# One loop over image pairs for the patch embedding and the first attention of a two-layer ViT

## The reference, cut to what matters

```python
p = x.reshape(n, C, NP, PS, NP, PS).transpose(0, 2, 4, 1, 3, 5).reshape(n, NP * NP, D_IN)
tokens = jnp.einsum('npd,hd->nph', p, W) + b
tokens = jnp.concatenate([cls, tokens], axis=1) + pos_embed[None]
...
h = _layernorm(tokens)                       # of each token, over its 192 features
q, k = h[:, :64], h[:, 64:]                  # the values are the keys
attn = softmax(einsum('bqc,bkc->bqk', q, k) * 0.25)
out = einsum('bqk,bkc->bqc', attn, k)
out = transpose(out, (0, 2, 1)).reshape(B, -1, 192) @ proj_w.T + proj_b
tokens = tokens + concatenate([out, k], axis=1)
```

## Time and profile before

| what | value |
|---|---|
| median of 3 runs | 2829.3 us (2827.83 to 2830.43) |
| the profiled execution, its own time | 2830.04 us |
| its span, first to last instruction | 2828.2 us |
| busy: PE / DVE / ACT / POOL, share of the span | 92% / 84% / 67% / 40% |
| TensorE clock granted, mean | 0.929 of full speed |

### The profile page before, as it was taken

How to read it: one execution, slowest core, us unless ns; L and a number is a source line. 1 busy time by engine, 2 the same in 40 slices (tenths; PEclk the granted TensorE clock), 3 DMA queues, 4 the chain that set the end, 5 groups by cost and what they waited for, 6 DMA issues and landing times. The chain is left out here.

```text
span 2828.2 us, 82965 instructions
## 1 busy us (share of the span) xinstructions
PE 2588.6 (92%) x27416; PEld 2173.2 (77%) x27416; DVE 2378.9 (84%) x5917; ACT 1904.5 (67%) x5750; POOL 1136.9 (40%) x1288
## 2 busy tenths in 40 slices
PE   5797888699999799999999999999999999997776
PEld 5796555477777588888888888888888888885554
DVE  6955666699999688888888888888888888887998
ACT  3343444333333388888888888888888888886998
POOL 5585333222222034334333433433333344344665
PEclk9897555599999999999999999999999999997999
DMA  9461000000000133333333333333333333330111
GB/s 286 137 187 52 0 0 0 0 1 0 0 0 0 27 79 78 73 68 77 69 72 77 77 71 70 77 68 74 77 77 70 71 75 68 75 78 9 42 40 47
DMA packets 181687, 173.31 MB, mean 61 GB/s; under 512 B 19064, under 2 KB 180290, under 8 KB 181379
## 3 DMA queue, kind: packets, MB, share of 16 engines
q1 hardware_dynamic: 181634, 172.64, 25.1%
HBM read 46.68 MB, written 9.68 MB: 20 GB/s over the span
## 5 line engine op out<-in xcount | busy, mean ns | idle before, releaser
L1183 POOL TENSOR_TENSOR b_pr<-b_pr,b_rinv 128x394 f32<-128x394 f32 (+1 forms) x768 | 625.7, 841 | 1008.4 <-DVE b_rinv L1141 1008.4
L1078 ACT ACTIVATE b_pr<-b_banks,b_nmx 128x197 f32<-128x197 f32 (+1 forms) x1536 | 625.0, 423 | 28.2 <-DVE b_nmx L1135 25.6
L1049 ACT ACTIVATE b_pt<-b_bank_t 128x394 f16<-128x394 f32 (+1 forms) x768 | 337.4, 493 | 203.5 <-PE b_bank_t L1014 203.3
L1135 DVE TENSOR_REDUCE b_nmx<-b_banks 128x2 f32<-128x394 f32 (+1 forms) x768 | 397.3, 558 | 64.7 <-PE b_banks L1004 56.5
L1106 DVE TENSOR_TENSOR b_pt<-b_bank_t,b_pt 128x394 f16<-128x394 f32 (+1 forms) x768 | 395.8, 556 | 18.3 <-ACT b_pt L1049 18.2
L988 PE MATMUL b_banks<-b_xt,wqkv 128*128 128x197 f16 x3840 | 373.6, 249 | 4.5 <-DVE b_xt L1106 2.2
L1014 PE MATMUL b_bank_t<-ident,b_pr 128*128 128x128 f32 (+3 forms) x3072 | 341.8, 253 | 3.1 <-DVE b_pt L1106 3.0
L988 PEld LDWEIGHTS b_banks<-b_xt,wqkv 128*128 128x128 f16 x3840 | 320.5, 98 | 25.7 <-issue 18.8
L1004 PE MATMUL b_banks<-b_kst,b_qst 128*128 128x197 f16 (+1 forms) x3072 | 326.9, 248 | 6.8 <-ACT b_pr L1078 5.4
L1078 ACT ACTIVATION_READ_ACCUMULATOR b_pr<-b_banks,b_nmx 128x1 f32 (+1 forms) x1536 | 315.5, 205 | 0.0
L1014 PEld LDWEIGHTS b_bank_t<-ident,b_pr 128*128 128x128 f32 (+3 forms) x3072 | 282.2, 142 | 43.2 <-issue 35.4
(11 more groups left out here) (175 smaller groups left out, 4657.4 us busy)
## 6 DMA issues: line engine op xcount, KB each, us to landing
b_qst<-b_qk SPq DMA_DIRECT2D x512, 147.8 KB, 2.5
b_kst<-b_qk SPq DMA_DIRECT2D x512, 73.9 KB, 2.3
patches<-in_x SPq DMA_DIRECT2D x64, 588.0 KB, 4.4
out<-z_res SPq DMA_DIRECT2D x32, 192.0 KB
out<-z_res SPq DMA_DIRECT2D x32, 103.5 KB
h<-in_wqkv SPq DMA_DIRECT2D x2, 1152.0 KB, 7.6
h<-in_w SPq DMA_DIRECT2D x2, 576.0 KB, 8.1
h<-in_fc SPq DMA_DIRECT2D x1, 768.0 KB
```

The source lines that it names most:

```text
L1049: return nc.scalar.activation(dst, src, ACT.Copy)
L1078: last = nc.scalar.activation(pr[n % 3][0:ROWS[c], c, e, :], banks[0:ROWS[c], c, e * SEQ:(e + 1) * SEQ], ACT.Exp, bias=nmx[n % 2][0:ROWS[c ...
L1135: v.reduce_max(nmx[n % 2][0:ROWS[c], c, :], banks[0:ROWS[c], c, 0:2 * SEQ].rearrange("p (e t) -> p e t", e=2), AX.X, negate=True).then_inc ...
L1183: last = nc.gpsimd.tensor_tensor(p, p, inv, ALU.mult)
```

## The change

`embed_patches` and `attention_0` become one function, `embed_attend`. Each engine has one list of steps for a round; a `'` behind a step means one pair ahead and each `^` one pair behind. A round makes both images of one pair (steps with 0 and 1: `h` the high parts on ACT, `l` the low parts on POOL, `E` the matmuls, `a` the addition of positions, `b` the statistics) and the attention steps of earlier pairs. Parts and token banks are one per image of a pair instead of four.

`norm_tables` is no longer called for this stage. In its place stand steps `r0` to `r14` on DVE for each pair, on tiles of 128 x 4: four `bn_aggr`, then a guess of the inverse root by integer arithmetic and three Newton steps, and the scale and offset for ACT. POOL no longer adds keys: ACT does it with an activation in place (`u`), `scale` 1 + 1/sigma (`u` for the 133 key rows of each of the two images, four activations). The projection's bias comes from one more matmul. The weight jobs stand after `a1` (or `a0`) of pairs 3, 5, 7, 8 to 10, 10, 12 and 14. More small loads stand ahead of the first image.

```diff
-        embed_patches(nc, A, S, n_img)
-        attention_0(nc, S, n_img)
+        embed_attend(nc, A, S, n_img)
...
+    PE_ORDER = "E0 t^^^^ x^^^ j^^^^^ m^^^^ E1 s^^^".split()
+    ACT_ORDER = ("u^^^ h0' k^^^ g^^^^ x^^ e^^^ h1'").split()
+    DVE_ORDER = ("o^^^^^ r8^^ r9^^ r10^^ t^^^^ r11^^ r12^^ r13^^ i^^^^ b1^ r14^^ n^^ s^^^^^^ r0^ a0 f^^^^^ "
+                 "r1^ r2^ r3^ m^^^ r4^ r5^ x^^ p^^^ b0 a1 r6^ r7^").split()
...
-        patches = [sb(f"patches{b}", [P, PATCH_K, SEQ]) for b in range(BUF)]
-        parts = [sb(f"parts{b}", [P, 2, PATCH_K, SEQ + 1], F16) for b in range(BUF)]
-        tokens = [ps(f"tokens{b}", [P, 512]) for b in range(BUF)]
+        patches = [sb(f"patches{q}", [P, PATCH_K, SEQ]) for q in range(4)]
+        parts = [sb(f"parts{m}", [P, 2, PATCH_K, SEQ + 1], F16) for m in range(2)]
+        tokens = [ps(f"tokens{m}", [P, 512]) for m in range(2)]
...
+                def low_parts(s, p, like):
+                    m = int(s[1])
+                    pool.wait_ge(patch_hi[m], p + 1)
+                    x = parts[m]
+                    nc.gpsimd.tensor_tensor(x[:, 1, :, 0:SEQ], patches[2 * (like % 2) + m][:], x[:, 0, :, 0:SEQ], ALU.subtract)\
+                        .then_inc(patch_split[m], 1)
...
+                    if kind == "h":
+                        act.wait_ge(loaded[2 * b + m], 8 * p + 16 - 8 * b)
+                        if later(p):
+                            act.wait_ge(made[m], p)
+                        copy(parts[m][:, 0, :, 0:SEQ], patches[2 * b + m][:]).then_inc(patch_hi[m], 1)
...
+                    elif kind == "u":
+                        act.wait_ge(xn_made, p + 1)
+                        act.wait_ge(norm[LAST_NORM], p + 1)
+                        for m in range(2):
+                            for c, rows in ((0, slice(NK1, P)), (1, slice(0, TAIL))):
+                                x, j = h[rows, 2 * p + m, c, :], 2 * m + c
+                                last = nc.scalar.activation(x, x, ACT.Identity, bias=my[b][rows, j:j + 1], scale=y1[b][rows, j:j + 1])
...
+                    if kind == "E":
+                        pe.wait_ge(patch_split[m], p + 1)
+                        if later(p):
+                            pe.wait_ge(taken[m], p)
...
+                        t.matmul(bank_r[:, 0:D], ones[:], pb_two[:], start=True, stop=False)
...
+                        else:
+                            dve.wait_ge(norm[n - 1], p + 1)
+                        if n == 1:
+                            last = v.tensor_scalar(var[b][:], mv[b][:, :, 1], EPS, None, ALU.add)
+                        elif n == 2:
+                            last = v.tensor_scalar(y[b][:].bitcast(I32), var[b][:].bitcast(I32), 1, None, ALU.logical_shift_right)
+                        elif n == 3:
+                            last = v.tensor_scalar(y[b][:].bitcast(I32), y[b][:].bitcast(I32), -1.0, ROOT_GUESS, ALU.mult, ALU.add)
+                        elif n in (4, 7, 10):
+                            last = v.tensor_tensor(t2[b][:], y[b][:], y[b][:], ALU.mult)
+                        elif n in (5, 8, 11):
+                            last = v.scalar_tensor_tensor(out=t2[b][:], in0=var[b][:], scalar=0.25 ** ((n - 5) // 3), in1=t2[b][:],
+                                                          op0=ALU.mult, op1=ALU.mult)
+                        elif n in (6, 9, 12):
+                            last = v.scalar_tensor_tensor(out=y[b][:], in0=t2[b][:], scalar=3.0, in1=y[b][:], op0=ALU.subtract, op1=ALU.mult)
+                        elif n == 13:
+                            last = v.tensor_scalar(y[b][:], y[b][:], -0.125, None, ALU.mult)
...
+                rounds(dve, DVE_ORDER, count, job, {"a0": {8 + n: take_turned_weights(n) for n in range(3)},
+                                                    "a1": {3: coefficients, 5: mask_weights, 7: low_fc, 10: quantised_steps, 12: quantised_weights,
+                                                           14: low_weights}}, first=2)
```

More of the change, by code:

```diff
@@ L123, in stage_tools, with ahead, later, rounds @@
     return sb, ps, sem
-def embed_patches(nc, A, S, n_img):
-    h, BUF, RAW_FROM, RAW_SIZE = S["h"], 4, 16, 48 * 2 * D
+def ahead(s):
+    return s.count("'") - s.count("^")
+def later(value):
+    return not (isinstance(value, int) and value <= 0)
+def rounds(eng, order, count, step, after=None, first=1):
+    after = after or {}
+    shifts = [ahead(s) for s in order]
+    tails = [k - ahead(s) for s in order for k in after.get(s.strip("'^"), {})]
+    def round_of(i, like):
+        for s in order:
+            if 0 <= like + ahead(s) < count:
+                step(s.strip("'^"), i + ahead(s), like + ahead(s))
+            if isinstance(i, int):
+                extra = after.get(s.strip("'^"), {}).get(i + ahead(s))
+                if extra:
+                    extra()
+    start = max([first - min(shifts)] + [k + 1 for k in tails])
+    turns = (count - max(shifts) - start) // 2
+    turns = turns if turns >= 2 else 0
+    for i in range(-max(shifts), start):
+        round_of(i, i)
+    if turns:
+        with eng.Fori(0, turns) as u:
+            for k in range(2):
+                round_of(2 * u + start + k, start + k)
+    for i in range(start + 2 * turns, count - min(shifts)):
+        round_of(i, i)
+def embed_attend(nc, A, S, n_img):
+    h, RAW_FROM, RAW_SIZE = S["h"], 16, 48 * 2 * D
+    count = n_img // 2
+    SP = SEQ + 1
+    SCALE = float(16) ** -0.5
+    LAST_NORM = 14
+    ROOT_GUESS = 1597463007.0
+    PE_ORDER = "E0 t^^^^ x^^^ j^^^^^ m^^^^ E1 s^^^".split()
+    ACT_ORDER = ("u^^^ h0' k^^^ g^^^^ x^^ e^^^ h1'").split()
+    DVE_ORDER = ("o^^^^^ r8^^ r9^^ r10^^ t^^^^ r11^^ r12^^ r13^^ i^^^^ b1^ r14^^ n^^ s^^^^^^ r0^ a0 f^^^^^ "
+                 "r1^ r2^ r3^ m^^^ r4^ r5^ x^^ p^^^ b0 a1 r6^ r7^").split()
     with ExitStack() as ctx:
@@ L185, in embed_patches @@
[L185 to L189, removed]
+        ones = sb("ones", [P, P], F16)
+        pb_high = sb("pb_high", [P, D], F16)
+        pb_rest = sb("pb_rest", [P, D])
@@ L196, in embed_patches @@
[L196 to L212, removed]
+                           (S["q1_bias"][:], A["b1"]), (S["q2_bias"][:], A["b2"])]
@@ L214, in embed_patches, with own @@
+        attention_loads = [(r_wo[:], A["wo"])] + [(r_qkv[:, k], A["wqkv"][:, k]) for k in range(2)]
+        def own(m):
+            return slice(m * NQ, (m + 1) * NQ)
         with nc.Block() as block:
@@ L280, in _ @@
                 act.wait_ge(tok_loaded, 16 * len(tok_loads))
[L281 removed]
+                copy(tok_w[:, 0], r_tok).then_inc(tok_hi, 1)
+                copy(S["pw"][:, 0], r_pw[:])
+                copy(S["ident16"][:], S["ident"][:])
+                copy(S["ident_b"][:], S["ident"][:]).then_inc(early_hi, 1)
                 act.wait_ge(zeroed, 1)
[L283 removed]
+                rounds(act, ACT_ORDER, count, job, {"h1": {7: masked_weights, 13: attention_weights}}, first=2)
@@ L297, in turn_weights @@
[L297 to L307, removed]
+                t = nc.tensor
@@ new lines, in turn_weights, with turn @@
+                def turn_weights(n):
+                    def turn():
+                        if n == 0:
+                            pe.wait_ge(masked, 2)
+                        else:
+                            pe.wait_ge(weights_taken, n)
+                        pe.wait_ge(taken[1], min(count, 8 + n))
+                        for f in range(2):
+                            part = slice((2 * n + f) * P, (2 * n + f + 1) * P)
+                            t.transpose(bank_t[:, f, 0:P], r_fp[:, 0, part], S["ident"][:])
+                            last = t.transpose(bank_t[:, f, P:D], r_fp[0:LO, 1, part], S["ident"][0:LO, 0:LO])
+                        if n == 2:
+                            for f in range(HC):
+                                last = t.matmul(bank_b[:, f:f + 1], bfc[:, f * P:(f + 1) * P], one[:], start=True, stop=True)
+                        last.then_inc(turned, 1)
+                    return turn
@@ L309, in _ @@
                 pe.wait_ge(tok_split, 1)
-                rounds(pe, multiply, [None, None, None, turn_weights])
+                rounds(pe, PE_ORDER, count, job, {"s": {4 + n: turn_weights(n) for n in range(3)}}, first=11 + min(ahead(s) for s in PE_ORDER))
             @block.vector
@@ L405, in _ @@
                 v.memset(S["stats"][:], 0.0)
+                for b in range(2):
+                    v.memset(mv[b][:], 0.0)
+                v.memset(ones[:], 1.0)
                 v.memset(g[:], 0.0)
```

524 lines of the change are left out of this document (267 added, 257 removed).

## The result

The changed kernel takes 2890.9 us (median of four runs, 2885.3 to 2892.8), against 2828.8 us before: a ratio of 1.022 (95% interval 1.020 to 1.023). It is slower by 62 us, where 12 us were forecast; the direction was forecast, the size was not.

The account below looks back on a forecast made before the run. DVE, stopped twice a round by POOL's subtractions, was taken as the bound: 22 + 60 + 393 + 32 + 48 = 555 us against 543.4, 12 us more, so 2841 us; range 2770 to 2895, likeliest case 2820 to 2865.

Parts of the forecast that it names:

- 11.1 us of work: DVE's own work in a joined round: attention 6.04, positions and statistics 2.46, tiny new operations 2.57 us.
- the two paths of the prediction: POOL's second subtraction on DVE: catching r7 costs 2.2 us; if r7 slips through, r8 loses 1.3.
- the same sum: Joined round on DVE: 11.1 us of work plus stops by POOL's two subtractions, 14.3 or 15.2 us.
- Rival B: Small DVE steps slip between POOL's subtractions or aren't stopped: round 11.1 to 13.5 us, 2764 us at 12.5; chance 0.20.
- the signs: Expected profile: DVE period 15 us, POOL busy near 150 us, DVE above 90% from 80 to 480 us, clock 0.75 to 0.95.
- the sign of D: Profile mark for Case D: DVE idles before the maximum for over 1 us, released by PE.
- the maximum comes up to 0.5 us late: PE's mixing, second image and score, with a cold start each round, delay DVE's maximum by up to 0.5 us.
- Case D: PE at low clock decides: mix, second image and score take 8.1 us, round 17, total 2896 us; chance 0.16.
- case A: The forecast: DVE bound, stopped twice per round, round 14.5 to 16 us, total 2841 us; chance 0.47.
- the weight jobs: 48: DVE's work preparing weights inside the joined loop: 52 us, less 4 where stops fall behind reciprocals, so 48.
- three filling rounds: Last of six rounds filling the joined loop before full rounds; the later ones were put at 11.1, 11.7 and 13.3 us.
- the last two full rounds and the emptying: End of the joined loop: full rounds at 15.1 us each, then six emptying rounds after the last image, 32 us.

Follow-up runs that it names:

- e3: The changed kernel with DVE's order changed so POOL's subtractions lie over operations they don't stop, and `u` behind the first patch copy on ACT: 2776.7 us.
- e1: The changed kernel with POOL's subtraction cut to two elements, leaving out the low parts (zero here): 2759.2 us.
- e2: The changed kernel with matmuls of ones added on PE, ten before the split of o and fourteen before the probabilities' copies: 2868.4 us.
- e4: The changed kernel with the turning of the MLP's weights moved from the second image's PSUM bank to the projection's bank: 2863.3 us.
- e8: The changed kernel with ACT's order alone changed, `u` behind the first patch copy, DVE's order kept: 2891.5 us.
- e7: The changed kernel with DVE's new order alone, `u` on ACT again ahead of the first patch copy: 2789.6 us.
- e5: The changed kernel with the new DVE and ACT order of e3 and the turning through the projection's bank of e4 together: 2755.8 us.

## Why the prediction was right and wrong

**Right.** DVE is the bound once it is not kept waiting: e3 runs at 11.14 with no wait, where the forecast had 11.1 us of work; in the change's own order that work is 10.71 (e1), 0.4 less than forecast. POOL's subtractions stop the root's steps. The step r6 loses 1.82 us (1.9 forecast); then r7 slips through and r8 loses 2.05, in every second round 1.7 (the two paths of the prediction gave 1.3 for r8 and 2.2 for r7). With PE at full clock (e2) the round is 14.67 us, and the prediction had 14.3 to 15.2 for the same sum. The Trainium skill ("SBUF — State Buffer", Who interferes with whom) tells of an exclusive lock held for the whole instruction and names no size. The trace agrees, for the 128 x 4 steps as well: 1.98 us against 0.16. Rival B, mild stops, falls. Of the signs, the granted clock (0.77 from 80 to 480 us) and POOL's busy time (160 us) came as said. DVE was busy 84% of that stretch and not above 90%, and the sign of D came too: DVE idle before the maximum for over 1 us, released by PE.

**The step that failed first: "the maximum comes up to 0.5 us late".** It came 1.4 us late (22.0 us over 16 maxima), which e2 took away. The step gave PE 5.8 us from the end of t to the maximum (8.1 to 13.9) for a piece of 4.2 us at full clock and one cold start of 1.5 us. What happened is that the second image's 36 matmuls, right behind PE's two waits, took 4.2 to 5.8 us where full clock gives 3.1, in every round. From DVE's copies to the maximum it was 6.0 to 7.6 us, of which DVE's own work is 5.4 to 5.7. The round is 16.06 us instead of 15.1. Case D's mechanism was thus at work inside case A, at half its size (16.06 lies midway between A's 15.1 and D's 17); the mistake was to price them as exclusive. No run here tests the sentence of the Trainium skill on transposes ("TensorE: Matmul & The Clock Gate", Part 4: PE-mode transpose): in e2 what was added were matmuls, and the transposes stayed.

**The term that was mis-sized: "the weight jobs: 48".** In the 12 first rounds there are 258.5 - 12 x 16.06 = 66 us above plain rounds. The sum counted what DVE does for the weights, and not that PE and DVE hand one PSUM bank back and forth for the turning; e4 removes 25 us of it and leaves 233.7 - 192.7 = 41; the forecast had 48 for all of it.

Set against the forecast on the same marks (from a round's first addition to its maximum I take the 2.4 us of 419.12 to 421.56), the 44 us by which the stage ended later (599.3 against 555) come apart so:

| part | forecast, us | measured, us | difference |
|---|---|---|---|
| until pair 0's maximum: 22 + 6.8 + 6.8 + 10.5 + 2.4 | 48.5 | 50.4 | +2 |
| three filling rounds, counted at 16.06 | 36.1 | 48.2 | +12 |
| weight jobs | 48 | 65.8 | +18 |
| 24 full rounds | 362.4 | 385.4 | +23 |
| the last two full rounds and the emptying: 30.2 + 32 - 2.4 | 59.8 | 49.4 | -10 |

The filling rounds were under-sized: the one without a weight job took 16.19 us, as long as a full one. Against them stands that the last two rounds of the 26 took 12.5 and 10.2 us and not 15.1; POOL has one subtraction left in the first of them and none in the second. That these two nearly cancel is luck. `u` was mis-sized as well, 2.21 us (543 ns each) where 1.2 to 1.6 were taken. In the change's DVE order e8 shows that its place doesn't decide the time (two stops of 1.98 and 2.27 us with POOL's operations back to back); in the new order it is worth 0.5 us a round (e7 against e3). The last 7 us of the 52 between 2841 and the profiled 2892.8 lie in the unchanged stages and stay open.

**What the change is worth.** The joined loop is not the loss: with the operations that read PSUM and the statistics beside POOL's subtractions (e3) and the turning in a free bank (e5), the stage takes 464 us against 543 before. What took it away is the order: a round of the change is DVE's 10.71 us, 3.87 of stops and 1.4 of clock (15.98, measured 16.06 in the mean), and the turning adds 25 us once.

## What to carry to other kernels

When long POOL operations run beside DVE, list which DVE operations they hold and put the others beside them; in this kernel the order of DVE and ACT was worth 114 us of 2891, and most of PE's clock came back by itself. Where a forecast has DVE late inside a ring with PE, add the clock's fall to it instead of keeping it as a separate case, and read how much of the lateness lands on the matmuls right behind PE's waits. For each job put into a loop, ask which PSUM bank it borrows and who queues for that bank behind it, before asking how long it takes.

## What the runs showed of the hardware that was not expected

A 128 x 4 operation of DVE, 0.16 us alone, is held for as long as POOL's subtraction still runs: it then lasts 1.98, 2.21, 2.27 and, met near the end, 0.56 us. The prediction took this from larger operations; here it is measured. That `bn_stats` and the additions from PSUM are not held was expected. New is that `RECIPROCAL` and `BATCH_NORM_AGGREGATE`, from SBUF to SBUF, ran at their usual 0.16 and 0.28 us (for three) in the middle of one, as did copies from PSUM (0.29) and o, which has one source in PSUM and another in SBUF (0.85 us for two). Four ACT operations in place on 64 or 69 partitions by 192 columns, scale and bias by pointer, take 2.21 us, while an exponential of 133 columns takes 0.37.
